# One GpSimd drain ahead of the last expert's scatters, in a one-core attention and mixture-of-experts kernel

## The reference

```python
x = x + xattn(layernorm(x), ctx, ctx, mask, ...)     # 16 heads of 16, 77 keys
x = x + ffn(layernorm(x), Wr, W1, W2)

# ffn: the best of 8 experts for each token, with a capacity
cap  = int(1.25 * B * S / E)                  # here 640 rows for each expert
pos  = jnp.sum(jnp.cumsum(onehot, axis=0) * onehot, axis=-1) - 1
kept = pos < cap
flat = idx * cap + jnp.minimum(pos, cap - 1)
disp = jnp.zeros((E * cap, D)).at[flat].add(t * kept[:, None])
h    = relu(einsum('ecd,edf->ecf', disp.reshape(E, cap, D), W1))
eout = einsum('ecf,efd->ecd', h, W2).reshape(E * cap, D)
out  = jnp.where(kept[:, None], eout[flat], t) * factor[:, None]
```

## Time and profile before

| what | value |
|---|---|
| median of 3 runs | 554.75 us (554.36 to 555.15) |
| profiled execution, its time | 556.13 us |
| its span, first to last instruction | 554.4 us |
| outside the span, the difference | 1.73 us |
| busy: PE, PEld, POOL, DVE, ACT | 84%, 57%, 34%, 37%, 27% of the span |

### The profile page before, as it was taken

One profiled execution on the slowest core, in us unless ns is written; L12 is line 12 of the kernel. 1 busy time (PEld: TensorE's weight loads), 2 busy tenths in 40 slices (PEclk: granted clock), 3 DMA queues, 4 the chain that ended last, 5 costly groups with the idle time before them and its releaser, 6 DMA issues.

```text
span 554.4 us, 7679 instructions
## 1 busy us (share of the span) xinstructions
PE 466.1 (84%) x2823; PEld 313.5 (57%) x2823; DVE 207.3 (37%) x590; ACT 152.3 (27%) x224; POOL 190.4 (34%) x306
## 2 busy tenths in 40 slices
PE   5797869699999999968243399999999999999991
PEld 2342234253434343423132288999989989899891
DVE  5853336355656565544242123112131121313110
ACT  0145515535554646344101111101001010111000
POOL 4671603408585766060626202111101111221221
PEclk9999979889999999968575589999999999999997
DMA  6992633614232333333402406015060060624000
GB/s 202 321 273 93 192 95 91 201 45 143 83 134 96 123 109 106 119 106 120 148 0 80 145 1 214 28 44 187 19 204 29 20 218 20 214 95 145 6 30 0
DMA packets 51658, 62.35 MB, mean 112 GB/s; under 512 B 4658, under 2 KB 41561, under 8 KB 51616
## 3 DMA queue, kind: packets, MB, share of 16 engines
q1 hardware_dynamic: 46560, 53.53, 30.4%
q0 software_dynamic: 3456, 7.26, 3.7%
q10 hardware_dynamic: 1600, 1.01, 0.7%
HBM read 32.17 MB, written 27.41 MB: 107 GB/s over the span
## 4 chain that ended last, share of the span: by engine, by line
PE 67%; DMA 9%; DVE 8%; SPq 7%; issue 4%; POOL 3%; ACT 1%; ACTq 0%; POOLq 0%; DVEq 0%
PE tps L1317 11%; PE wk L1327 10%; PE tps L1337 10%; PE wk L1345 9%; PE wk L1185 6%; SPq L399 6%; PE wk L1097 5%; PE nat L1117 5%; DMA attn_mem<-rsum 4%; PE tps L1139 3%; PE wk L1169 3%; DMA strips<-shared 2%; DVE rowmax L807 2%; DVE attn_mem L836 2%; PE nat L1305 1%
## 5 line engine op out<-in xcount | busy, mean ns | idle before, releaser
L588 POOL DMA_INDIRECT out_x<-attn_mem,dest x40 | 39.0, 975 | 198.6 <-DVE attn_mem L1014 195.8
L623 ACT ACTIVATE shared<-tps,mask_key 77x1024 f32<-77x1024 f32 x64 | 67.5, 1104 | 28.9 <-PE tps L1143 28.9
L807 DVE TENSOR_REDUCE rowmax<-nat 128x8 f32<-128x616 f32 x58 | 46.3, 798 | 51.6 <-PE nat L1117 50.6
L1117 PE MATMUL nat<-kblk,qT 64*128 64x308 f32 x232 | 47.0, 481 | 16.5 <-DVE rowmax L807 16.5
L1317 PE MATMUL tps<-shared,w_sb 128*128 128x256 f32 x256 | 59.7, 393 | 0.6 <-ACT shared L679 0.6
L1327 PE MATMUL wk<-w_sb,shared 128*128 128x256 f32 x256 | 57.7, 379 | 0.0
L1337 PEld LDWEIGHTS tps<-shared,w_sb 128*128 128x128 f32 x480 | 56.0, 192 | 0.8
L1337 PE MATMUL tps<-shared,w_sb 128*128 128x128 f32 x480 | 56.0, 275 | 0.0
L1317 PEld LDWEIGHTS tps<-shared,w_sb 128*128 128x128 f32 x256 | 50.7, 198 | 8.4 <-issue 1.0
L1345 PE MATMUL wk<-w_sb,shared 128*128 128x256 f32 x240 | 54.3, 379 | 0.0
L1327 PEld LDWEIGHTS wk<-w_sb,shared 128*128 128x128 f32 x256 | 48.1, 190 | 6.3
(11 more groups left out here) (136 smaller groups left out, 522.8 us busy)
## 6 DMA issues: line engine op xcount, KB each, us to landing
w_sb<-in_w SPq DMA_DIRECT2D x16, 1024.0 KB, 8.4
strips<-shared SPq DMA_DIRECT2D x32, 256.0 KB, 3.7
slot_rows<-zeros SPq DMA_DIRECT2D x1, 5200.0 KB, 25.7
x_sb<-slot_rows SPq DMA_DIRECT2D x8, 650.0 KB
x_sb<-in_x SPq DMA_DIRECT2D x8, 512.0 KB, 8.9
attn_mem<-strips SPq DMA_DIRECT2D x32, 128.0 KB
attn_mem<-rsum SPq DMA_DIRECT2D x64, 64.0 KB
out_x<-base SPq DMA_DIRECT2D x8, 512.0 KB, 3.1
```

What stands on the lines that cost most here:

```text
L588: pool.indirect_dma_start(out_rows, bass.IndirectOffsetOnAxis(ap=dest[n % 2][:, c:c + 1], axis=0), y_sb[n % 2][:, c, :], None, bounds_chec ...
L623: act.activation(probsT[0:SK, r % 2, 2 * i:2 * i + 2, :], tps[0:SK, 2 * i:2 * i + 2, :], ACT.Exp, bias=mask_key[:, g // GPB:g // GPB + 1]) ...
L807: dve.tensor_reduce(rowmax[:, j, :, m, :], nat_heads(g, k), AX.X, ALU.max).then_inc(rowmax_ready, 1)
L1117: last = pe.matmul(dst, qT[g % 2][of, m, j * P:(j + 1) * P], kblk[of, b, m, :, :].rearrange("p (i r) k -> p i (r k)", i=2), start=True, st ...
```

## The change

GpSimd's sequencer runs one more instruction, a drain. It stands at the start of the last expert's turn (n = 7), behind the 67th scatter of the program (32 of the first stage, 35 of the experts 0 to 6) and ahead of its waits for `dest_ready` and for the last expert's first tile. `next_expert(n)` is None for n = 7 only. Five scatters follow it. No other engine's code changes, and nothing is moved or removed.

```diff
             for n in range(E):
+                if not next_expert(n):
+                    pool.drain()
                 for c in range(SC):
                     if c == 0:
                         wait(pool, dest_ready, n + 1)
```

## The result

The changed kernel takes 548.42 us in the median of 4 runs (547.78 to 550.39), against 554.95 us for the kernel before in 4 runs (554.36 to 555.57). The ratio is 0.9888, with a 95% interval of 0.986 to 0.9916, so the gain is between 4.7 and 7.8 us. The forecast was 549.3, a gain of 5.4.

What follows compares the result with a forecast made beforehand. GpSimd's final drain, 5.957 us while four engines wait at the barrier, was taken to set the end; shrinking it to 0.58 or 0.41 gains 5.38 or 5.54, so 554.75 - 5.4 gives 549.3 us, range 548.6 to 551.0.

Steps and rivals of the forecast that it cites:

- The final drain is bookkeeping for each software DMA since the last drain: GpSimd's drain at the program's end: its 5957 ns settle all 72 software DMAs in proportion; 80 in 100.
- f and u: Drain cost, f + 72u = 5.957 us: fixed part f, 0 to 0.174 (first drain, memset included); u per DMA, 0.0803 to 0.0827.
- the two ends of 0.41 and 0.58: Final drain with five DMAs left: 0.58 us if f = 0.174, 0.41 us if f = 0.
- The early drain is hidden: Before the last expert's scatters: 5.55 us for 67 DMAs fits GpSimd's 6.8 us idle time, costing nothing in time.
- the cover: Time after 520.29 in which the early drain delays nothing on the path: until 540.0, or 19.7 us.
- The landing wait: Early drain may first await the scatter of 519.32: ends at 527.3 with median landing 2.4, 531.8 with longest 6.9.
- Nothing takes its place: Program end: last scatter's landing at 548.0 and some 0.4 us of branch and barrier come next; nothing gives the gain away.
- The sum: Whole kernel: span from 554.4 to 549.0 us, profiled execution from 556.13 to 550.75, plain time 549.3.
- 0.4 us of scatter between runs: Spread allowed either way around the forecast of 548.9 to 549.9 us.
- A bounded list: Rival, final drain: only C DMAs remain listed; 550.8 us for C = 16, 552.6 for C = 8; 8 in 100.
- A cost that isn't handed over: Rival, final drain: walks all 72 DMAs anyway or pays some 5.8 us once; 554.7 us, no change; 9 in 100.
- A drain that stops VectorE: Rival, last expert: early drain holds VectorE, shifting the end 3.5 to 5 us; 558.3 to 559.8 without gain; 3 in 100.

## Why the prediction was right

**The final drain is bookkeeping for each software DMA since the last drain.** Right, and shown: ten lengths of the list between 1 and 72 lie on one line to within 0.02 us, the list is emptied by a drain (41 ns behind another), and half the rows in each DMA change nothing. What the bookkeeping consists of isn't shown.

**f and u.** The fixed part was set too high and the part for each too low: f at 0.174 where the runs show 0.04 to 0.06, u at 0.0803 where they show 0.0820. The final drain with five DMAs came to 0.465 and not 0.58, inside the two ends of 0.41 and 0.58 that the text kept. The choice of the end f = 0.174 was the weaker one, as that row had a memset in it. For the early drain the choice hardly mattered: any f in the range gives 5.54 or 5.55 us for 67 DMAs, so that agreement says nothing about f.

**The early drain is hidden.** Right: 5.55 us from the scatter's row, forecast 5.55, ending 0.4 us ahead of the tile that GpSimd waits for (523.0 and 523.41). The idle time ahead of the fourth tile nearly covers a drain of 5.80 us as well: the scatter behind it was 0.4 us late. That the cover at the place of the change reaches to 540.0, as the prediction has it, was not tested. Past the edge, ahead of the last scatter, the whole gain is gone. The landing wait that the prediction added in front of the bookkeeping was not added there: the last scatter landed 2.1 us from its start, and the drain still ended 5.56 us after its row, the time for 67 DMAs alone.

**Nothing takes its place.** Right: the last scatter's landing and GpSimd's last wait are the end, with 0.2 us of branch ahead of the drain.

**The sum.** 5.49 us by the profiles, 5.4 forecast. The medians differ by 6.5 us and the ratio gives 6.2, with an interval that holds 5.5. What is beyond 5.5 I take to be spread, for these reasons: it lies ahead of the drain, and the repeated profile of the changed kernel doesn't show it. The runs made beside each other point the same way. Take the median span less the tail: 543.8 for the changed kernel, 544.8 for the kernel before, and 544.8, 545.2 and 546.0 for the drain ahead of the first expert, of the last scatter and of the fourth tile. The last two do just what the kernel before does up to the last expert's scatters, and come out later all the same. It isn't shown, though: the changed kernel's ratio was 0.9888 and 0.9889 in two sets of runs, and 0.9887 with the second drain added, each a little below the 0.990 that the drain alone gives, and each with an interval that holds 0.990. The term that was mis-sized is the one for this spread: I wrote 0.4 us of scatter between runs, from the three runs shown, and the 30 runs of the kernel before reach over 7.6 us. If it is spread, this is why the median fell just below the range. It weakens one more step: from a difference of 1.4 us between one profiled execution and three others I concluded that at least 4.6 us of the drain were real, and executions differ by more than that anyway. The gain of the medians is the better evidence.

**The rivals.** A bounded list: fallen, since 64 and 72 DMAs lie on the line of the small numbers. A cost that isn't handed over: fallen with the 465 ns. A drain that stops VectorE: L1006 took 0.69 us in the middle of it. By the Trainium skill's sentence in "PSUM — Partial Sum Buffer", Engine vs sequencer instructions, that a drain waits for the engine to go fully idle, both drains should have been near nothing; of GpSimd's drains behind software DMAs none agrees, and only the one with an empty list was that short, 41 ns.

## What to carry to other kernels

Read what stands behind the last busy row: a drain at the block's end is in no busy time, and here it was 1% of the kernel. On GpSimd its cost grows by 0.082 us for each software DMA since the last drain, so in a kernel with many of them it is worth trying one drain in a late idle stretch of GpSimd, long enough for it and past the big loads: here that moved nearly all of it off the path. Fewer software DMAs save the same for each. Where the row of a drain starts ahead of the engine's last work, count it from the end of that work, and compare such a small gain by the tail from a fixed event, not by spans.

## What the runs showed that I had not expected

A GpSimd drain behind scatters that run beside weight loads took 5.1 to 5.9 us from the last scatter's row with only five DMAs on its list, ending 0.24 us after that scatter had landed. Landings were 5.9 to 6.6 us there, and 2.1 where nothing was loading.

Executions of one program differ in the time at which the experts start. GpSimd's last wait was over at 548.0 and 553.5 in the two profiles of the kernel before, and at 545.2 and 547.8 in the two of the changed one, with the tails equal to 0.01 us. What makes the first stage vary this much was not looked into.
